# One VectorE product per query tile instead of three, in a four-block transformer kernel on one core

## The reference

```
q_hk = (hidden_q @ Wq.T).reshape(Bv, Sv, H, K)
q_big = jnp.einsum('bshk,hkq->bshq', q_hk, w_kc_q)
q_big = _apply_rope(q_big, sin_q, cos_q)          # x * cos + rotate_half(x) * sin
kv_r = _apply_rope(kv_c, sin_k, cos_k)
q_r = jnp.einsum('bshq,hqr->bhsr', q_big, W_qr)
k_r = jnp.einsum('bld,hdr->bhlr', kv_r, W_kr)
attn = softmax(einsum('bhsr,bhlr->bhsl', q_r, k_r))
ctx = einsum('bhsl,bld->bhsd', attn, kv_r) -> w_kc_kv -> Wo
```

## Time and profile before

| | before |
|---|---|
| median of 3 runs | 511.13 us (508.57 to 515.8) |
| span of the profiled execution | 507.1 us |
| PE busy | 448.3 us (88%) |
| DVE busy | 382.8 us (75%) |
| ACT busy | 282.7 us (56%) |
| POOL busy | 216.8 us (43%) |

### The profile page before, as it was taken

One profiled execution on the slowest core, in us unless ns is written; L12 is line 12 of the kernel. 1 busy time (PEld: TensorE's weight loads), 2 busy tenths in 40 slices (PEclk: granted clock), 3 DMA queues, 4 the chain that ended last, 5 costly groups with the idle time before them and its releaser, 6 DMA issues. The chain is left out here.

```text
span 507.1 us, 11890 instructions
## 1 busy us (share of the span) xinstructions
PE 448.3 (88%) x4610; PEld 341.6 (67%) x4610; DVE 382.8 (75%) x881; ACT 282.7 (56%) x626; POOL 216.8 (43%) x281
## 2 busy tenths in 40 slices
PE   3966998889899999898998999897859999999994
PEld 3435675358677777787787777786637777777774
DVE  4459998568578888887897687885557778788892
ACT  2677687574355666544656455555317455566560
POOL 3266151002222222523554256523323567888364
PEclk9997899899899999999999999998869999999999
DMA  8893006900720000000070001000103765677633
GB/s 269 259 341 65 1 1 198 365 6 1 214 79 2 3 1 2 2 1 1 1 233 23 1 1 45 23 1 8 45 1 119 219 174 135 160 207 217 183 42 40
DMA packets 37721, 46.76 MB, mean 92 GB/s; under 512 B 7584, under 2 KB 33056, under 8 KB 37472
## 3 DMA queue, kind: packets, MB, share of 16 engines
q1 hardware_dynamic: 32912, 40.82, 25.3%
q0 software_dynamic: 4224, 4.79, 6.0%
q10 hardware_dynamic: 528, 0.38, 0.3%
HBM read 40.14 MB, written 8.55 MB: 96 GB/s over the span
## 5 line engine op out<-in xcount | busy, mean ns | idle before, releaser
L583 POOL TENSOR_TENSOR lw<-lw 128x512 f32<-128x512 f32 x48 | 60.7, 1270 | 110.0 <-DVE lw L1197 108.9
L891 ACT ACTIVATE lw<-psum,nmax 128x256 f32<-128x256 f32 x128 | 59.2, 469 | 18.8 <-DVE nmax L1252 18.8
L1751 PE MATMUL psum<-lp 128*128 128x256 f16 x576 | 69.7, 276 | 0.0
L898 ACT ACTIVATE lw<-psum 128x512 f16<-128x512 f32 x64 | 38.2, 597 | 51.9 <-PE psum L1851 51.9
L1257 DVE TENSOR_TENSOR lw<-psum,lw 128x512 f16<-128x512 f32 x64 | 43.7, 682 | 29.9 <-ACT lw L898 29.8
L1751 PEld LDWEIGHTS psum<-lp 128*128 128x128 f16 x576 | 54.7, 99 | 7.0 <-issue 0.5
L2014 PE MATMUL psum<-lw,se 128*128 128x320 f16 x384 | 55.6, 303 | 2.3 <-issue 1.8
L973 ACT ACTIVATE lw<-psum,b1w 128x320 f16<-128x320 f32 x64 | 33.7, 527 | 37.8 <-PE psum L2014 37.8
L681 POOL DMA_INDIRECT out_x<-lw,tslot x24 | 44.5, 1855 | 19.6 <-DMA out_x<-lw,tslot 7.3
L1851 PE MATMUL psum<-identf,lw 128*128 128x128 f32 x256 | 41.4, 285 | 12.6 <-DVE lw L1257 11.0
L2014 PEld LDWEIGHTS psum<-lw,se 128*128 128x128 f16 x384 | 37.0, 99 | 19.7 <-issue 2.5
(11 more groups left out here) (247 smaller groups left out, 983.0 us busy)
## 6 DMA issues: line engine op xcount, KB each, us to landing
se<-in_w SPq DMA_DIRECT2D x16, 1024.0 KB, 8.3
dispatch<-in_empty SPq DMA_DIRECT2D x4, 662.5 KB, 9.6
lw<-dispatch SPq DMA_DIRECT2D x8, 265.0 KB
lp<-in_Wq SPq DMA_DIRECT2D x2, 1024.0 KB, 9.9
se<-in_WoT SPq DMA_DIRECT2D x1, 2048.0 KB, 12.2
lp<-in_w_kc_q SPq DMA_DIRECT2D x2, 768.0 KB, 10.2
x_sb<-in_x SPq DMA_DIRECT2D x2, 512.0 KB, 6.0
se<-in_gate_wT SPq DMA_DIRECT2D x1, 1024.0 KB, 8.8
```

What stands on the lines that cost most here:

```text
L583: nc.gpsimd.tensor_tensor(rope[:, c % QT, :], t1[:, c % 2, :], t2[:, c % 2, :], ALU.add)\
L891: A_(e_sb[:, n % 2, st * S:(st + 1) * S], bank[3 + n % 2][:, st * S:(st + 1) * S], ACT.Exp, bias=nmax[:, n % 2, st:st + 1], accum_out=esum ...
L898: A_(at[0][:, n % 2, :], bank[5][:, :], ACT.Copy).then_inc(a_at, 1)
L1751: ins = M(tile_bank(c)[:, half * S:(half + 1) * S], m1[w][:, kc, half, col:col + P], (yth, ytl)[a][:, kc, b * S:(b + 1) * S], start=(n == ...
```

## The change

`turn(c)` is one instruction. It reads the bank twice (a broadcast axis of two, step 0, ahead of the 512 values), multiplies it by a table `rotq` that holds for each tile the 512 cosines and then the 512 sines, and writes 1024 values into `t12`, whose slot holds the straight product and then the crossed one. The halves are not exchanged any more: the sine table's halves are stored in reverse order, so each crossed product lies in the half of its source. `rotate(c)` exchanges them, by reading the crossed product with its two halves of 256 in reverse order (a negative step over an axis of two). `v_t2` is gone. The tables arrive by one transfer of the same bytes instead of two, and POOL does not wait for them itself any more.

```
-            sp.dma_start(cosq, A["cosq"]).then_inc(d_t, 16)
-            sp.dma_start(sinq, A["sinq"]).then_inc(d_t, 16)
+            sp.dma_start(rotq, A["rotq"]).then_inc(d_t, 16)
...
-            pool.wait_ge(d_t, 32)
-
             def rotate(c):
 
-                pool.wait_ge(v_t2, 2 * c + 2)
                 pool.wait_ge(v_t1, c + 1)
                 if c >= QT:
                     pool.wait_ge(p_qz, c // QT)
-                nc.gpsimd.tensor_tensor(rope[:, c % QT, :], t1[:, c % 2, :], t2[:, c % 2, :], ALU.add)\
-                    .then_inc(g_rope, 1)
+                straight, crossed = [t12[:, c % 2, k, :].rearrange("p (h s) -> p h s", h=2) for k in range(2)]
+                nc.gpsimd.tensor_tensor(rope[:, c % QT, :].rearrange("p (h s) -> p h s", h=2), straight, crossed[:, ::-1, :],
+                                        ALU.add).then_inc(g_rope, 1)
...
                 if c == 0:
-                    dve.wait_ge(d_t, 32)
+                    dve.wait_ge(d_t, 16)
                 dve.wait_ge(p_qb, c + 1)
                 if c >= 2:
                     dve.wait_ge(g_rope, c - 1)
-                r = tile_bank(c).rearrange("p (h s) -> p h s", h=2)
-                sn = sinq[:, c % QT, :].rearrange("p (h s) -> p h s", h=2)
-                o = t2[:, c % 2, :].rearrange("p (h s) -> p h s", h=2)
-                V.tensor_tensor(o[:, 0, :], r[:, 1, :], sn[:, 0, :], ALU.mult).then_inc(v_t2, 1)
-                V.tensor_tensor(o[:, 1, :], r[:, 0, :], sn[:, 1, :], ALU.mult).then_inc(v_t2, 1)
-                V.tensor_tensor(t1[:, c % 2, :], tile_bank(c)[:, :], cosq[:, c % QT, :], ALU.mult).then_inc(v_t1, 1)
+                V.tensor_tensor(t12[:, c % 2], tile_bank(c).unsqueeze(1).broadcast_to([P, 2, 2 * S]), rotq[:, c % QT],
+                                ALU.mult).then_inc(v_t1, 1)
```

More of the change, by code:

```diff
@@ L107, in program @@
         tabs = lp([2 * QT * 2 * S])
-        cosq, sinq = [tabs[:, i * 2 * QT * S:(i + 1) * 2 * QT * S].rearrange("p (a b) -> p a b", a=QT) for i in range(2)]
+        rotq = tabs.rearrange("p (c k s) -> p c k s", c=QT, k=2)
         kvT0 = lp([T])
@@ L149, in program @@
         w2([4 * 256])
-        t1 = w2([2, 512])
-        t2 = w2([2, 512])
+        t12 = w2([2, 2, 512])
         rope = w2([QT, 512])
@@ L292, in program @@
         p_kr, a_kr, v_krl = sem("p_kr"), sem("a_kr"), sem("v_krl")
-        p_qb, v_t1, v_t2, g_rope = sem("p_qb"), sem("v_t1"), sem("v_t2"), sem("g_rope")
+        p_qb, v_t1, g_rope = sem("p_qb"), sem("v_t1"), sem("g_rope")
         p_qz, a_qz, v_qz = sem("p_qz"), sem("a_qz"), sem("v_qz")
@@ L2053, in tables @@
     both = [np.stack([t[:, at].T, t[:, at + HALF].T], axis=1) for t in (cos, sin)]
-    cosq, sinq = [(b.reshape(QT, P, 2 * S).transpose(1, 0, 2) / np.float32(WS)).astype(np.float32) for b in both]
+    both[1] = both[1][:, ::-1, :]
+    rotq = np.stack([b.reshape(QT, P, 2 * S).transpose(1, 0, 2) / np.float32(WS) for b in both], axis=2).astype(np.float32)
     ks, kc = rot(S, DC)
@@ L2061, in tables @@
     return {
-        "cosq": cosq, "sinq": sinq, "kcos": kcos, "ksin": ksin, "identf": eye, "ident16": eye.astype(np.float16),
+        "rotq": rotq, "kcos": kcos, "ksin": ksin, "identf": eye, "ident16": eye.astype(np.float16),
         "identb": eye.astype(mybir.dt.np(BF16)), "trib": np.triu(np.ones((P, P), np.float32), 1).astype(mybir.dt.np(BF16)),
```

## The result

| | before | after |
|---|---|---|
| median | 513.32 us | 508.87 us |
| lowest, highest | 508.57, 517.38 | 503.95, 511.12 |
| ratio of the times | | 0.9916, 95% interval 0.9886 to 0.9945 |
| span of the profiled execution | 507.1 us | 508.5 us |

The change gains 4.3 us (2.8 to 5.9). The time, 508.9 us, lies 0.3 us from the forecast, but the kernel before came out 2.2 us slower here than in its first three runs, so the gain is about twice the 1.9 us that the sum gave. Both intervals hold a gain of 2.8 to 4.0 us. The forecast's 1.9 us, a ratio of 0.9963, lie outside the first interval and inside the second. All ratios leave out executions that took over 1.5% more than the fastest of their kernel, one of 1464.63 us in e9_tile3_only among them.

What follows compares the result with a forecast made beforehand. PE was taken as the bound, busy 194.4 of 208 us in the change's stage. Updates 0.9, counts 0.6, first group's end 0.3 and first split 0.13 sum to 1.9 us: 511.1 - 1.9 = 509.2 us, range 504.9 to 513.

Steps and rivals of the forecast that it cites:

- DVE's saving: DVE's turn of each tile: one product lasting 1.21 us, 1.13 us between starts, saving 0.13 us a tile, 6.2 us over 48.
- POOL: POOL's rotations with the reversed read: 0 to 0.09 us more each, taken as 0.03, hidden by 1.12 us of cover.
- Ordinary groups give nothing: Groups without update or count: a shorter turn only lengthens DVE's idle time before at_low, which waits for ACT's copy.
- The updates: The three updates (n = 19, 35, 51), where PE waits for at_low: 0.3 us gained each, 0.9 us.
- The first group's end: PE's 1.04 us wait for at_low, behind two turns and L1261, at the first group's end: 0.3 us gained.
- The counts: The counts at n = 28 and 44, where PE waits 0.48 us for the last turn: 0.3 us each, 0.6 us.
- with the clock granted in full: The stretch from 138 to 346 us, holding the change, was read as having PE's full clock.
- The split ahead of the first scores: The fourth tile's turn right ahead of the first latent split, for which the first scores wait: 0.13 us gained.
- Nothing gets through: Rival: each named PE wait is replaced by one for ACT; 511 us, within 1 us of before; chance 0.30.
- More gets through: Rival: earlier exponentials and closed short PE pauses, or whole durations freed; 4 to 6 us gained; chance 0.12.
- POOL the bound: Rival: reversed read doubles a rotation to 2.54 us, PE waits 1.16 us at 15 latents; 526 us; chance 0.05.
- DVE slower: Rival: the second pass over the bank costs DVE time beyond 1.26 us a tile; 512 to 514 us; chance 0.05.

Runs made afterwards that it cites:

- e9_tile3_only: Changed kernel with only the fourth tile (c = 3) as one DVE instruction, the other 47 as three; ratio 0.9992 to the kernel before.
- e4_two: Changed kernel with two DVE instructions of 512 values a tile instead of one of 1024; ratio 0.9987 to the kernel before.
- e3_three: Changed kernel with three DVE instructions a tile again, keeping the joined table and POOL's reversed read; ratio 1.0011 to the kernel before.
- e2_after_again: The changed kernel, unedited, timed and profiled a second time; ratio 0.9954 to the kernel before.
- e12_extra_product: Changed kernel with one more DVE product of 256 values per tile, written where nobody reads it; ratio 1.0166 to the kernel before.
- e1_before_again: The kernel before, unchanged, timed against itself and profiled a second time; ratio 1.0015.
- e6_loop: Changed kernel with the first six tiles as three DVE instructions, the loop's 42 as one; ratio 0.9955 to the kernel before.
- e5_first6: Changed kernel with only the first six tiles as one DVE instruction, the other 42 as three; ratio 0.9951 to the kernel before.
- e7_rotate_twice: Changed kernel with POOL making each rotation's addition twice, once into an unread buffer; ratio 1.0666 to the kernel before.
- e8_split_first_before: Kernel before with the first latent split moved ahead of the fourth tile's turn in DVE's order; ratio 0.9932 to the kernel before.
- e10_after_split_first: Changed kernel with the first latent split moved ahead of the fourth tile's turn; ratio 0.9827 to the kernel before.
- e11_update_later: Changed kernel with first latent split ahead of the fourth turn, and updates and statistics one head later, behind at_low; ratio 1.0008 to the kernel before.

## Why the prediction was right or wrong

That the time came out 0.3 us from the forecast is luck: the kernel before was 2.2 us slower here than in its first three runs, and the sum lacked a term. The terms one by one.

**DVE's saving: right.** 1.213 us measured for 1.21, 1.13 us from start to start for 1.13. The bank is read a second time at the rate of the first. The start distances say 0.13 us saved a tile, and the two halves of 0.60 us in e4_two say it again. In the Trainium skill, the terms of "VectorE: DVE Perf Modes" let the next operation issue only when the pipe is empty, which gave the estimate of 0.31 us a tile; the trace does not agree, and the measurement decides.

**POOL: right, at the low end.** 1.272 us against 1.27, and e3_three with the reversed read alone is 1.001. The 0.03 us a rotation that I took could have been nothing. By section 3.1 of the "GPSIMD Engine Reference" of the Trainium skill, addresses cost GpSimd no cycles of their own; here the trace agrees.

**Ordinary groups give nothing: right.** 40.67 us before, 40.67 after for three of them; DVE's idle time takes all of it, 0.54 to 0.92 us.

**The places on the path.** The updates were to give 0.3 us each and give 0.31 to 0.39; PE's wait there is 1.10 us, where I had expected 1.1:

```profile
211.15 0.63 PE L1843 MATMUL psum<-identf,lw 128*128 128x128 f32 x4 [1.10 <-DVE lw L1249]
```

The first group's end gives 0.39 instead of 0.3. The counts give 0.11 and 0.15 instead of 0.3 each: of the wait of 0.48 us for the turned tile 0.09 us is left in e2_after_again, but the transposes behind the next scores then wait 0.12 us for at_low, which has itself waited for ACT's copy, as in the rival:

```profile
237.08 0.69 DVE L1249 TENSOR_TENSOR lw<-psum,lw 128x512 f16<-128x512 f32 x1 [0.27 <-ACT lw L894]
```

In before at_low had no such wait there.

One place I missed: at n = 24, 40 and 56, in the stretches 6 to 7, 10 to 11 and 14 to 15, PE's product for the expert logits waits for the same tiles, since it writes bank 0. DVE and PE in order of time, before, and then in e2_after_again:

```profile
222.56 0.68 DVE L1197 TENSOR_TENSOR lw<-psum,lp 128x512 f32<-128x512 f32 x1
...
222.82 0.51 PE L1865 MATMUL psum<-lp,lw 128*128 128x64 f16 x12
...
223.38 1.03 PE L1911 MATMUL psum<-gwt,se 128*128 128x8 f32 x8
```

```profile
220.02 1.21 DVE L1188 TENSOR_TENSOR lw<-psum,lp 128x1024 f32<-128x1024 f32 x1
...
221.20 0.51 PE L1857 MATMUL psum<-lp,lw 128*128 128x64 f16 x12
...
221.55 1.04 PE L1903 MATMUL psum<-gwt,se 128*128 128x8 f32 x8
```

The logits start 0.56 us behind the context's start before and 0.35 us after: 0.2 us each, 0.6 us. The view of PE's waits has no row for it, since the products before it still count as busy. It is to be found by reading what `route_logits` waits for. By chance the errors nearly cancel: the loop was to give 1.8 us and gives 2.3.

**The step that failed: "with the clock granted in full".** The split ahead of the first scores was put at 0.13 us. The wait did become 0.12 us shorter, but the stretch became 1.9 us shorter, since the lower clock that follows this wait with three instructions a tile does not follow it with one. Between the first two latents, over all kernels:

| PE's wait ahead of the first scores | kernels | granted clock of the stretch |
|---|---|---|
| 2.25 us | e12_extra_product | 0.89 |
| 2.04, 2.05 us | before, e1_before_again, e3_three, e6_loop | 0.88 each |
| 1.98 us | e4_two | 1.00 |
| 1.92 us | after, e2_after_again, e5_first6, e7_rotate_twice, e9_tile3_only | 1.00 each |
| none seen | e8_split_first_before, e10_after_split_first, e11_update_later | 1.00 each |

Five of five above 2 us, none of nine below. Each is one execution, and this is no bound of the chip: in e7_rotate_twice waits of 1.82 us were followed by the lower clock, and in e9_tile3_only one of 2.09 us was not. How much of this gain is in the timed runs is not shown: e5_first6 (0.9951) and e8_split_first_before (0.9932) speak for it, e9_tile3_only (0.9992) doesn't, and e4_two (0.9987) leaves no room for all of it. The mean granted clock of the timed executions is on record too. One fall as in the first profile of before, 3.4 us at half, would be 0.0034 of it. Against the kernel before on the same chip it is higher by 0.0007 to 0.0037 in the six kernels whose profile has no fall there (e2, e4, e5, e8, e9, e10), and lower by 0.0001 to 0.0015 in the three with one (e1, e3, e6). That points the same way, but the scatter of each mean is 0.001 to 0.002. The first measured gain, 4.3 us, needs it; the second, 2.3 us, would do with the loop alone.

**The rivals.** "Nothing gets through" (within 1 us) is excluded by the stretches and the first interval; the second reaches down to a gain of 0.7 us. "More gets through", 4 to 6 us, is where the first measurement lies, but not by either of its mechanisms. "POOL the bound" would have been worse than I priced it, since I took only the lateness and not what a late addition and a waiting PE run into. "DVE slower" is excluded by the 1.213 us.

## What to carry to other kernels

Making one elementwise instruction of three saves what lies between instructions (0.13 us of 1.26 here, by start distances and not by durations), and it comes out only where that engine's queue is the last thing waited for: 2.3 us of the 5.5 that the loop's 42 tiles save on DVE. Before a change at a place where PE waits some 2 us is priced, look at the granted clock of the stretch behind the wait, from the wait on and not from a round number: a tenth of a microsecond there went with 1.8 us more in the profiles. And ask of the longest such wait whether an exchange in the waiting queue takes it away (e8_split_first_before, 3.4 us for one moved line), before work is made shorter.

## What the runs showed of the hardware

- A GpSimd addition of 512 values that ran beside a VectorE instruction with both inputs in SBUF took 2.24 us instead of 1.27, and the VectorE instruction 1.39 instead of 1.21 us (e7_rotate_twice). The specifications in the "GPSIMD Engine Reference" of the Trainium skill name this contention without a figure; the trace agrees.
- A negative step over an axis of two costs GpSimd nothing (1.272 us), nor does a step of 0 over a PSUM bank cost VectorE anything (1.213 us for 1024 values).
- PE's clock fell to 0.50, from 2.4 to 1.2 GHz, behind some waits of 1.7 to 3.3 us in the middle of steady work and not behind others of up to 2.09 us. Where it fell, it cost about 1.6 us on top of the wait: 11.33 us of PE instead of 9.67 for the first stretch's 109 products, and 16.07 us instead of 14.49 for e9_tile3_only's stretch from latent 10 to 11.
- ACT's idle time ahead of the 14th latent copy is 2.7 to 3.5 us, for something remote, in five profiles: the first after the change, e9_tile3_only, e10_after_split_first, e11_update_later and e12_extra_product. It is 1.07 us in both profiles of before. The first four also have 0.3 to 1.0 us ahead of the 10th, where before has 0.01. The four experiments with these pauses are all those that ran on one chip; none of those on the two other chips has a remote wait there. So the pauses go with the chip or the time of the run at least as well as with the kernel; their cause is open.
